# An adaptive-norm transformer block on one core: half of one weighted sum moved ahead of the side products

## The reference

```
h = layernorm(x) * (1 + ca) + sa                       # sa, ca, ga, sb, cb, gb from silu(c) @ wmod
qkv = (h @ Wqkv.T + bqkv).reshape(B, 16, S, 24)        # 16 "heads" of 1024 rows x 8, cut from 64 tokens each
attn = softmax(q @ k.T / sqrt(8)) @ v                  # 1024 x 1024 scores for each of the 64 (batch, head) pairs
x = x + ga * (attn.reshape(B, S, 128) @ Wo.T + bo)
h = layernorm(x) * (1 + cb) + sb
p = softmax(h @ router_w.T); two best of 8 experts
x = x + gb * sum over the two of (h @ expert_e + p_e) * w_e
```

## Time and profile before

| what | value |
|---|---|
| three runs | 556.68, 556.86, 558.76 us (median 556.86) |
| the profiled execution's own time | 557.98 us |
| its span, first to last instruction | 556.1 us |
| mean granted TensorE clock | 0.994 of full speed |
| PE busy | 519.1 us (93%) |
| ACT busy | 494.8 us (89%) |
| DVE busy | 362.8 us (65%) |
| POOL busy | 219.2 us (39%) |
| exponentials (line 547) | 512, from 23.8 to 532.9 us |

### The profile page before, as it was taken

How to read it: one execution, slowest core, us unless ns; L and a number is a source line. 1 busy time by engine, 2 the same in 40 slices (tenths; PEclk the granted TensorE clock), 3 DMA queues, 4 the chain that set the end, 5 groups by cost and what they waited for, 6 DMA issues and landing times. The chain is left out here.

```text
span 556.1 us, 14357 instructions
## 1 busy us (share of the span) xinstructions
PE 519.1 (93%) x4064; PEld 215.3 (39%) x4064; DVE 362.8 (65%) x1271; ACT 494.8 (89%) x571; POOL 219.2 (39%) x429
## 2 busy tenths in 40 slices
PE   7488889999999999999999999999999999999983
PEld 6233333334343434343433333343434343433352
DVE  4435457677867666677767667677676666664466
ACT  1279989999999999999999999999999999998962
POOL 1223233344443334444443343444433344443335
PEclk9999999999999999999999999999999999999997
DMA  4573333333333333333333333333333332333010
GB/s 100 128 199 90 89 96 78 77 97 88 89 90 89 96 98 84 76 78 93 88 90 90 98 93 83 72 88 91 88 89 95 98 86 65 91 96 84 17 32 14
DMA packets 85497, 48.44 MB, mean 87 GB/s; under 512 B 61508, under 2 KB 76240, under 8 KB 85456
## 3 DMA queue, kind: packets, MB, share of 16 engines
q1 hardware_dynamic: 70162, 43.07, 30.0%
q10 hardware_dynamic: 15294, 4.82, 3.8%
HBM read 32.91 MB, written 14.94 MB: 86 GB/s over the span
## 5 line engine op out<-in xcount | busy, mean ns | idle before, releaser
L547 ACT ACTIVATE probs<-ps_scores 128x1024 f32<-128x1024 f32 x512 | 485.8, 1028 | 42.9 <-DMA q_scr<-qk_parts 19.6
L735 PE MATMUL ps_attn<-probs,values 128*32 128x512 f32 x2048 | 248.1, 599 | 0.4 <-issue 0.4
L717 PE MATMUL ps_scores<-query_stack,key_stack 32*128 32x512 f32 x1024 | 130.7, 500 | 17.5 <-ACT probs L547 11.4
L717 PEld LDWEIGHTS ps_scores<-query_stack,key_stack 32*128 32x128 f32 x1024 | 49.4, 183 | 167.9 <-ACT probs L547 164.1
L422 POOL TENSOR_SCALAR var_eps<-moments 128x1 f32<-128x1 f32 x64 | 12.3, 192 | 222.7 <-DVE moments L1078 149.5
L735 PEld LDWEIGHTS ps_attn<-probs,values 128*32 128x32 f32 x2048 | 54.0, 109 | 110.5 <-issue 110.3
L765 PE MATMUL ps_side<-experts_gated,h2T 128*128 (+1 forms) x228 | 74.7, 409 | 0.0
L1067 DVE RECIPROCAL sums_inv<-sums 128x128 f32<-128x128 f32 x32 | 30.5, 952 | 32.5 <-DMA attnT<-a_scr 32.5
L1074 DVE TENSOR_TENSOR x<-ps_side,x_gated 128x128 f32<-128x128 f32 x31 | 9.0, 292 | 60.8 <-PE ps_side L765 57.2
L1150 DVE TENSOR_TENSOR weighted<-ps_side,coef 128x256 f32<-128x256 f32 x114 | 46.5, 408 | 2.4 <-PE ps_side L765 2.4
L471 POOL TENSOR_TENSOR mix<-weighted 128x512 f32<-128x512 f32 x31 | 39.7, 1280 | 0.0
(11 more groups left out here) (129 smaller groups left out, 498.9 us busy)
## 6 DMA issues: line engine op xcount, KB each, us to landing
key_stack<-k_scr SPq DMA_DIRECT2D x128, 128.0 KB, 2.7
query_stack<-q_scr SPq DMA_DIRECT2D x121, 64.0 KB, 2.2
q_scr<-qk_parts SPq DMA_DIRECT2D x188, 32.0 KB, 2.0
k_scr<-qk_parts SPq DMA_DIRECT2D x64, 64.0 KB, 1.7
a_scr<-attn ACTq DMA_DIRECT2D x126, 18.0 KB
sums<-a_scr SPq DMA_DIRECT2D x32, 64.0 KB, 2.1
attnT<-a_scr SPq DMA_DIRECT2D x32, 64.0 KB, 2.2
out_dram<-out_all ACTq DMA_DIRECT2D x29, 64.0 KB, 1.8
```

The source lines that it names most:

```text
L547: nc.scalar.activation(probs[:, k % RING, g, :], ps_scores[:, slot(k, g), :], ACT.Exp, scale=SCALE)\
L717: mm = nc.tensor.matmul(out_, key_stack[p0:p0 + 32, parity, 2 * k:2 * k + 2, :].rearrange("p j r -> p (j r)"), query_stack[p0:p0 + 32, par ...
L735: mm = nc.tensor.matmul(ps_attn[q:q + 32, :], values[:, parity, g, k, :], probs[:, k % RING, g, h * HALF:(h + 1) * HALF], start=(k == 0), ...
```

## The change

`weigh` gets a range of columns. The even block that is due (k - 2) is weighed in two halves of the query columns: columns 0 to 255 of each strip directly behind `scores(k)`, in front of the side products, and columns 256 to 511 where all of it stood before, behind `scores(k + 1)`. The waits of `weigh` (for `attn_saved` and `values_done` where k is 0, for the probabilities always) go with the first half; the count on `pv_done` goes with the second. Odd blocks, and the last two blocks of the last tile, are weighed whole as before.

```
-            def weigh(t, t1, parity, k):
-
-                if k == 0:
-                    reached(pe, ev["attn_saved"], t)
-                    reached(pe, ev["values_done"], t1)
+            def weigh(t, t1, parity, k, columns=slice(0, HALF)):
+
+                if columns.start == 0:
+                    if k == 0:
+                        reached(pe, ev["attn_saved"], t)
+                        reached(pe, ev["values_done"], t1)
+                    for g in range(G):
+                        reached(pe, probs_ready[k][g], t1)
                 for g in range(G):
-                    reached(pe, probs_ready[k][g], t1)
                     for h in range(2):
                         q = 32 * (2 * g + h)
-                        mm = nc.tensor.matmul(ps_attn[q:q + 32, :], values[:, parity, g, k, :],
-                                              probs[:, k % RING, g, h * HALF:(h + 1) * HALF],
-                                              start=(k == 0), stop=(k == KT - 1), tile_position=(0, q))
-                mm.then_inc(pv_done[k], 1)
+                        mm = nc.tensor.matmul(ps_attn[q:q + 32, columns], values[:, parity, g, k, :],
+                                              probs[:, k % RING, g, h * HALF + columns.start:h * HALF + columns.stop],
+                                              start=(k == 0 and columns.start == 0), stop=(k == KT - 1), tile_position=(0, q))
+                if columns.stop == HALF:
+                    mm.then_inc(pv_done[k], 1)

+            def weigh_past(at, parity, before, k, columns):
+
+                if k >= 0:
+                    weigh(at[0], at[1], parity, k, columns)
+                elif before:
+                    weigh(at[-1], at[0], 1 - parity, KT + k, columns)
+
             def between_sides(at, parity, before, k, exact):
                 scores(at[0], at[1], parity, k, exact)
-                for past_k in (k - 3, k - 2):
-                    if past_k >= 0:
-                        weigh(at[0], at[1], parity, past_k)
-                    elif before:
-                        weigh(at[-1], at[0], 1 - parity, KT + past_k)
+                weigh_past(at, parity, before, k - 3, slice(HALF // 2, HALF))
+                weigh_past(at, parity, before, k - 2, slice(0, HALF))
                 if k + 1 < KT:
                     scores(at[0], at[1], parity, k + 1, exact)

                 for k in range(0, KT, 2):
+                    weigh_past(at, parity, before, k - 2, slice(0, HALF // 2))
                     if k == 0:
                         drained3(at, before, after, 0)
```

## The result

The changed kernel takes 589.3 us (median of 5, 587.88 to 590.3) against 556.68 us (556.59 to 558.76) for the kernel before: 1.057 times as long, 95% interval 1.0543 to 1.0597, or 32.6 us more. Forecast were 584.4 us and a range of 568 to 600. The profiled execution took 589.3 us with a span of 587.5, against 557.98 and 556.1.

What follows compares the result with a forecast made beforehand. PE was taken to bound the tile, with 15.43 us of work and 0.32 idle. 24 x 1.02 = 24.5, loop edges 4.0 and outer tiles -1 gave +27.5 us: 584.4 us on the median, range 568 to 600.

Steps and rivals of the forecast that it cites:

- h: Time half a sum takes on PE ahead of a side: 0.50 us, from 2 x 0.22 plus 0.06 for the passage.
- Step 1: Odd-to-even block step on PE loses half a sum: 2.29 to 1.86 us, four times a tile.
- Step 2: Even-to-odd block step on PE gains half a sum of 0.50 us, including 0.06 for passage from column strips to side.
- Rival C: Full array drain at the added passage from column strips to side: 14 us more, 598 us; chance 0.11.
- Step 3: First half of weigh(0), behind scores(2), waits for the copy, itself delayed by side0: PE stands 1.06 us per tile.
- Step 4: Side1, scores(3) and ACT queue behind that wait; nothing makes it good: tile 16.77 us, +1.02.
- other moved waits are long met: Waits for block k - 2's probabilities and the tile's values_done, moved with the first half, cost nothing.
- Step 5: PE's sequencer arrives late at the loop edge, 2.1 to 2.29 us after scores(7): 0.33 us in 12 rounds, +4.0.
- forecast A: The forecast itself: wait of about 1.06 us in each tile, 584.4 us, own range 577 to 592; chance 0.70.
- Rival B: Copy isn't delayed, as c_x1 starts as before: wait 0.56 us, 15 us less, 569.5 us; chance 0.12.
- Rival D: Copy comes in time, the wait vanishes and PE's idle 0.32 us is won: 550 or 554 us; chance 0.04.
- Rival E: Short groups of 256 columns expose their weight loads: 56 us more, 640 us; chance 0.03.

Runs made afterwards that it cites:

- experiment 6: Kernel before with only the half sum at k = 0 moved, placed behind side0 and in front of scores(1): 556.25 us, ratio 0.9974.
- experiment 2: Changed kernel with the copy of the sums placed ahead of x1hat on DVE: 577.29 us, ratio 1.0361 to the kernel before.
- experiment 3: Changed kernel with the half at k = 0 left behind the odd scores (halves moved at k = 2, 4, 6): 578.50 us, ratio 1.0390 to the kernel before.
- experiment 9: Kernel before plus only a PE wait for attn_saved behind scores(2), in front of side1; no sum split or moved: 569.00 us, ratio 1.0206.
- experiment 1: Changed kernel with block 0's sum left whole behind the odd scores (halves moved at k = 0, 4, 6): 568.59 us, ratio 1.0207 to the kernel before.
- experiment 4: Changed kernel with the half at k = 6 left behind the odd scores (halves moved at k = 0, 2, 4): 583.73 us, ratio 1.0480 to the kernel before.
- experiment 10: Changed kernel with every even sum still cut into two halves, but both left behind the odd scores: 564.49 us, ratio 1.0137 to the kernel before.
- experiment 5: Changed kernel with a half moved at k = 0 only, in front of side0, all else as in the kernel before: 566.40 us, ratio 1.0163 to it.

## Why the prediction was right

- **What bounds the kernel.** Right. PE's 0.32 us of idle time in a tile is what balance could bring, and experiment 6, which fills the larger part of it, gains 0.07 us a tile. But "all else on PE is work" missed another 0.07, inside side3, where PE waits for POOL's squares in the kernel before:

```profile
275.40 0.80 POOL L430 TENSOR_TENSOR squares<-qkT 128x256 fp32r<-128x256 f32 x1
...
276.25 0.39 PE L671 MATMUL ps_side<-head_sum,squares 128*128 128x16 f32 x2
```

 The squares end at 276.20. In the changed kernel, with side3 0.57 later, that wait is gone, and the step 6-7 came out at 2.15 as forecast although h was larger.
- **Step 1, odd to even, 1.86.** Measured 1.86.
- **Step 2, h = 0.50.** Too small: 0.57. The exit from column strips costs the same 0.11 into a side as into scores, the upper end of my 0 to 0.11; and the first short group takes 0.24, as the first long one took 0.02 more than the others. That is 0.07 more in each of four places, 0.26 a tile or 6 us. I halved a mean step and took the middle between two ends, where the nearer row (sum to scores, 0.11) was at hand. Rival C falls: its full drain would be 0.18, and in tile 16 the side starts at 294.74, before the end of the last short group as the profile gives it (294.17 + 0.64 = 294.81). The Trainium skill ("TensorEngine Tiling (Array Packing)", Key Properties) has a change of tiling mode drain TensorE. The traces agree in kind and show 0.11 on the way out of column strips and some 0.02 on the way in; that these are the drain is not shown.
- **Step 3, the wait.** The mechanism is shown by experiments 2, 3 and 9, and by PE's idle 23.4 us. Its size, 1.06, is 0.99 in even tiles and 0.76 in odd ones, 0.19 too much in the mean or 4.5 us. I had read a single tile and put the copy's start down to x1hat; that tile 16 came out within 0.01 is in part luck, as said above. In the kernel before, the copy's group on the page is:

```profile
L1061 DVE COPY attn<-ps_attn 128x512 f32<-128x512 f32 x31 | 21.4, 691 | 10.1 <-PE ps_attn L735 10.1
```

 Its idle time was ended by PE's last sum, in 19 of 31 cases. The copy stood at 4.04 in nearly all tiles because of that sum (in experiment 6, where the sum ends 0.07 earlier, it starts at 3.97 in even and odd tiles alike), while x1hat was early in every second tile (tile 17: x1 1.51 after `scores(0)`, tile 16: 1.67). Once the sum came earlier, the difference between the two tiles of the loop's round came out.
- **Step 4, nothing makes it good.** Right: experiment 9 gives a wait of 0.45 and a tile of +0.43. But "other moved waits are long met" was incomplete. Side1's wait for x1hat is not moved and yet is pushed behind its date, by 0.21 to 0.45 us. It cost nothing on top of the copy's wait and 8 us when that is taken away (experiment 1).
- **Step 5, loop edge.** 0.33 was taken; the steps of 2.16 to 2.21 against 1.86 give 0.30 to 0.35, and experiment 4, which leaves the whole step long, gets 0.28 a tile back. The reason I gave, a fixed number of instructions ahead, fell in experiment 10; what the traces show is a chain of control steps of 1.6 us that starts 0.45 to 0.6 behind `scores(7)`, and what sets its start is open.
- **The sum.** h was 6 us too small and the wait 4.5 us too large, so two errors partly met. What lies outside the loop was put at -1, give or take 3, and came to +1.5: tiles 0 to 3 take 0.8 less, tiles 28 to 31 1.8 more and the tail 0.4 more. In tiles 28 to 31 the step 2-3 is about as long as in the loop (2.89 to 3.54), so that their lighter sides did not pay for the wait. Single gaps do not make the difference, since both kernels have two there (steps of 3.31 and 3.34 before, 3.10 and 2.86 after). 27.5 + 1.4 (the loop's tiles) + 2.5 (the outer ones) is the span's 31.4; the rest of the medians' 32.6 is spread between runs. The lower end of forecast A's own range is added up wrongly: with no loop edges and no passage cost its terms give 574.6 (584.4 - 4.0 - 24 x 4 x 0.06) or less, not 577.

Rival B (copy not delayed) falls by experiment 3, which had to take the half out of side0's way to make it true. Rival D would have needed the copy to start before the sum that it copies was done; experiment 2 shows the earliest start, 3.97. Rival E falls by experiment 10. By kind of cost, the +1.24 us of a tile are: wait for the copy 0.88; four splits, 4 x 0.57 less 4 x 0.43 and less what PE had stood idle before (0.32, and 0.07 inside side3: 1.65 + 0.57 - 2.15), together 0.17; the step into the next tile 0.19.

## What to carry to other kernels

A piece of work moved forward on an in-order engine takes its waits along: look up when each producer is ready, and recompute that date with what the move itself delays in front of it, since here the same half sum that was to wait for the copy had made the copy later. Behind the wait that one finds there may be a second one; taking the first away showed it, and experiment 5 a third. And when an engine is 99% busy, fill its idle 0.2 us at the spot where it is idle, behind whatever other engines are waiting for (behind side0: -0.3%, in front of it: +1.6%).

## What the runs showed of the hardware

- Leaving four column strips (128 x 32) costs 0.11 us beyond the last group's time, into row strips and into the whole array alike (0.54 against 0.43, and 0.33 against 0.22). Entering them costs about 0.02: the first short group takes 0.24 and not 0.22.
- Groups of four fp32 matmuls in column strips take 0.22 us at 256 columns and 0.43 at 512: halving them costs nothing by itself.
- At this loop's edge, with two branches (0.21 us for the loop's own, line 252) and a loaded flag, PE's sequencer needs 1.6 us for its control steps. They start 0.45 us after the last scores, so that the next scores come no sooner than 2.16 to 2.21 after them, even where the array would be free at 1.86. With 16 more queued instructions they start at about 0.6.
